# Decoder layer with a 4-bit feed-forward on one core: code tiles loaded before the rows of y, and the last batch's normalized rows made one at a time

## The reference

```python
x = x + self_attention(layernorm(x))      # 32 query heads, 16 key heads, head dim 32, causal
x = x + cross_attention(layernorm(x))     # keys and values: ctx, 4 x 64 tokens x 256, 8 kv heads, mask
x = x + down(silu(gate(n)) * up(n))       # n = layernorm(x), 1024 -> 3584 -> 1024
# gate, up, down: NF4[code] * absmax, one code per int32, one absmax per 64 codes
```

## Time and profile before

| | |
|---|---|
| median of 3 runs | 2753.37 us (2748.1 to 2753.88) |
| profiled execution | 2752.58 us, of which the span is 2750.8 us |
| busy over the span | PE 94%, DVE 75%, ACT 56%, POOL 45% |
| attention part, to the first feed-forward product | 993.7 us |
| feed-forward | 1757 us, 14 groups |
| mean granted TensorE clock | 0.971 of 2.4 GHz |

### The profile page before, as it was taken

One profiled execution on the slowest core, in us unless ns is written; L12 is line 12 of the kernel. 1 busy time (PEld: TensorE's weight loads), 2 busy tenths in 40 slices (PEclk: granted clock), 3 DMA queues, 4 the chain that ended last, 5 costly groups with the idle time before them and its releaser, 6 DMA issues.

```text
span 2750.8 us, 52702 instructions
## 1 busy us (share of the span) xinstructions
PE 2580.6 (94%) x18536; PEld 1402.1 (51%) x18536; DVE 2068.4 (75%) x2860; ACT 1548.4 (56%) x2762; POOL 1235.4 (45%) x1032
## 2 busy tenths in 40 slices
PE   5899999999975479999999999999999999999999
PEld 3567677776754444444444444444444444444444
DVE  5656777778778768878787878878787878778773
ACT  3566666666665347556464746556464746455550
POOL 2356667777765334343342424343342424243340
PEclk9999999999986689999999999999999999999999
DMA  5242443343343032111121112111111112111113
GB/s 195 93 147 93 119 131 120 98 148 107 107 154 97 28 115 69 39 58 50 45 61 38 61 46 61 38 53 53 46 59 40 61 40 66 38 53 53 46 35 122
DMA packets 155421, 212.23 MB, mean 77 GB/s; under 512 B 34576, under 2 KB 86288, under 8 KB 155280
## 3 DMA queue, kind: packets, MB, share of 16 engines
q1 hardware_dynamic: 155280, 210.31, 24.4%
HBM read 163.98 MB, written 44.56 MB: 76 GB/s over the span
## 4 chain that ended last, share of the span: by engine, by line
PE 83%; DVE 5%; DMA 3%; issue 3%; POOL 2%; ACT 2%; SPq 1%; ACTq 0%; DVEq 0%; POOLq 0%
PE bank L1728 42%; PE pair L1747 21%; PE bank L969 6%; PE bank L975 2%; PE pair L1026 2%; PE bank L997 2%; PE bank L929 1%; PE bank L1064 1%; DMA nat_parts<-nat 1%; PE pair L1049 1%; PE pair L1053 1%; PE pair L1051 1%; POOL arena L812 1%; PE bank L999 1%; PE pair L1028 1%
## 5 line engine op out<-in xcount | busy, mean ns | idle before, releaser
L277 DVE TENSOR_TENSOR w_l<-w_l 128x512 f32<-128x512 f32 x1008 | 918.9, 961 | 17.3 <-ACT w_l L260 17.2
L260 ACT ACTIVATE w_l<-proj 128x512 f32<-128x512 int32 x1008 | 592.3, 620 | 413.3 <-DVE w_l L277 299.2
L1728 PE MATMUL bank<-w_h,q_rows 128*128 128x512 f16 x2688 | 584.9, 379 | 1.2 <-issue 1.2
L1747 PE MATMUL pair<-k_rows,arena 128*128 128x512 f16 x2688 | 582.4, 379 | 0.0
L812 POOL TENSOR_TENSOR arena<-p,arena 128x512 f16<-128x512 f32 x320 | 371.5, 1169 | 230.6 <-ACT arena L1244 229.7
L1728 PEld LDWEIGHTS bank<-w_h,q_rows 128*128 128x128 f16 x2688 | 262.5, 98 | 318.4 <-issue 1.3
L1747 PEld LDWEIGHTS pair<-k_rows,arena 128*128 128x128 f16 x2688 | 262.6, 98 | 317.6
L299 POOL TENSOR_TENSOR q_rows<-x1T,q_rows 128x512 f16<-128x512 f32 x112 | 144.1, 1287 | 508.0 <-ACT q_rows L266 508.0
L257 ACT ACTIVATE w_l<-proj,bounds 128x512 f32<-128x512 int32 x336 | 231.9, 713 | 244.5 <-DVE w_l L277 209.8
L294 POOL TENSOR_TENSOR x1T<-x1T,nat 128x512 f32<-128x512 f32 x168 | 265.6, 1581 | 199.8 <-DVE x1T L283 199.8
L1438 DVE TENSOR_REDUCE block_max<-bank 128x4 f32<-128x512 f32 x320 | 218.9, 687 | 168.9 <-PE bank L999 165.4
(11 more groups left out here) (131 smaller groups left out, 3756.1 us busy)
## 6 DMA issues: line engine op xcount, KB each, us to landing
proj<-in_codes SPq DMA_DIRECT2D x168, 256.0 KB, 3.0
nat<-in_scales SPq DMA_DIRECT2D x336, 128.0 KB, 2.9
nat_parts<-nat SPq DMA_DIRECT2D x48, 256.0 KB, 2.1
q_rows<-nat_parts SPq DMA_DIRECT2D x96, 128.0 KB, 2.7
x_unit<-in_x SPq DMA_DIRECT2D x64, 128.0 KB, 2.7
x<-x_unit SPq DMA_DIRECT2D x64, 128.0 KB, 2.4
xn<-in_x SPq DMA_DIRECT2D x14, 512.0 KB, 4.3
x_row<-x SPq DMA_DIRECT2D x14, 512.0 KB, 4.6
```

The costliest lines, as they stand in the source:

```text
L260: op = self.nc.scalar.activation(self.t.line[:, m, :], self.t.codes[:, slot, :], ACT.Copy, scale=slope, bias=intercept)
L277: self.nc.vector.tensor_tensor(line[:, n + 2, :], line[:, n, :], line[:, n + 2, :], ALU.max)\
L1728: mm = nc.tensor.matmul(bank[(GATE, UP)[kind] + n % 2][:, :], w[:, chunk, kind, P * c:P * c + P], t.fT[nb][:, :, part, c, :], start=(m == ...
L1747: mm = nc.tensor.matmul(down_bank[r % 2][:, half, :], h[:, m // 3, rows], w[:, m // 3, cols], start=(m == 0), stop=(m == 5))
```

## The change

Four edits.

1. `load_late_rows` becomes `load_late_row(n)`: one of the five transfers at the start of each of the steps 59, 61, 63, 65, 67.
2. The twelve loads of y leave the end of `attention`. `load_y(sp, r)` keeps their waits, and `feed_forward` calls it twice behind the codes and scales of each of k = 1 to 6.
3. A table `LATE_ROWS` gives each of the nine late rows its iterations for stats, normalization and turn. ("cross", 3, 0) stays at -2; rows 1, 2, 3 go to turns at n = 2, 5, 9. The five third rows keep their iterations, except that the last of batch 2 has all three one later. The order of the nine, and the slot of `xn` of each (they alternate), follow from the table. SP's load of ("third", 2, 3) goes from n = 1 to n = 2.
4. In an iteration, PE transposes a row behind that iteration's scores, weighing and x_turn (cross rows were transposed ahead of the scores). ACT's high parts stand behind the exp. DVE does the low parts of a row, then a normalization, then stats, all behind mask, low part and division; before, the cross rows' stats, normalization and low parts stood ahead of them.

```diff
@@ tiles' steps, order and slots
+    LATE_STEPS = (59, 61, 63, 65, 67)
-    LN_ORDER += [("cross", B - 1, rt) for rt in range(QT)] + [("third", B - 2, QT - 1)]
-    LN_ORDER += [("third", B - 1, rt) for rt in range(QT)]
+    LATE_ROWS = [(("cross", B - 1, 0), (-2, -2, None)), (("cross", B - 1, 1), (0, 1, 2)),
+                 (("cross", B - 1, 2), (3, 4, 5)), (("third", B - 2, 3), (4, 5, 6)),
+                 (("third", B - 1, 0), (6, 7, 8)), (("cross", B - 1, 3), (7, 8, 9)),
+                 (("third", B - 1, 1), (10, 11, 12)), (("third", B - 1, 2), (14, 15, 16)),
+                 (("third", B - 1, 3), (18, 19, None))]
+    LN_ORDER += [at for at, turns in LATE_ROWS]
+    LATE_SLOTS = {at: n % 2 for n, (at, turns) in enumerate(LATE_ROWS)}
-    def third_rt(n):
-        for i, at in enumerate(((3, 4, 5), (6, 7, 8), (10, 11, 12), (14, 15, 16), (18, 19, 20))):
-            if n in at:
-                return at.index(n), LN_ORDER[len(LN_ORDER) - 1 - QT + i]
-        return None, None
+    def late_rows(stage, n):
+        return [at for at, turns in LATE_ROWS if turns[stage] == n]
@@ SP
-        def load_late_rows():
-            sp.wait_ge(turned_stored, 16 * len(STORED_ORDER))
-            sp.wait_ge(proj_done, NP * B)
-            for n, (what, b, i) in enumerate(LATE_ORDER):
-                sp.dma_start(t.fT[b][:, i, :, :, :].rearrange("p a c n -> p (a c n)"), dram["fT"][n, :, :])\
-                    .then_inc(rows_loaded, 16)
+        def load_late_row(n):
+            if n == 0:
+                sp.wait_ge(turned_stored, 16 * len(STORED_ORDER))
+                sp.wait_ge(proj_done, NP * B)
+            what, b, i = LATE_ORDER[n]
+            sp.dma_start(t.fT[b][:, i, :, :, :].rearrange("p a c n -> p (a c n)"), dram["fT"][n, :, :])\
+                .then_inc(rows_loaded, 16)
...
+            if s in LATE_STEPS:
+                load_late_row(LATE_STEPS.index(s))
...
-            if s == tiles.FIRST_STEP:
-                load_late_rows()
             load_tiles(tiles.in_step(tiles.CODES, s), tiles.in_step(tiles.SCALES, s))
...
         for n in range(-2, NX + 2):
             load_tiles(tiles.in_turn(tiles.CODES, n), tiles.in_turn(tiles.SCALES, n))
-            if n == 1:
+            if n == 2:
                 load_row("third", B - 2, QT - 1)
-        sp.wait_ge(x_added, NX * B)
-        for r in range(10):
-            sp.dma_start(t.y[r], x2_row(r)).then_inc(y_loaded[0], 16)
-        sp.wait_ge(ln_turned, 2 * len(LN_ORDER))
-        for r in range(10, 12):
-            sp.dma_start(t.y[r], x2_row(r)).then_inc(y_loaded[1], 16)
...
+    def load_y(sp, r):
+        if r == 0:
+            sp.wait_ge(x_added, NX * B)
+        if r == 10:
+            sp.wait_ge(ln_turned, 2 * last + 2)
+        sp.dma_start(t.y[r], dram["x2"][r // QT, P * (r % QT):P * (r % QT) + P, :]).then_inc(y_loaded[r // 10], 16)
...
-        def group(i, last, first=0):
-            for k in range(first, last_k(last)):
+        def group(i, last, first=False):
+            for k in range(1 if first else 0, last_k(last)):
                 tiles.load_codes(sp, i, k)
                 tiles.load_scales(sp, i, k)
+                if first and k <= 6:
+                    for r in range(2 * k - 2, 2 * k):
+                        rest.load_y(sp, r)
@@ POOL
-        ln_root(LN_AT["cross", B - 1, 1])
...
-            if n in (0, 1):
-                ln_root(LN_AT["cross", B - 1, n + 2])
...
-            stage, at = third_rt(n)
-            if stage == 0:
+            for at in late_rows(0, n):
                 ln_root(LN_AT[at])
@@ PE
-                if n in (0, 1, 2):
-                    turn(n + 1, 0)
-                    turn(n + 1, 1)
...
-                stage, at = third_rt(n)
-                if stage == 2:
-                    for half in range(2):
-                        turn(at[2], half, *at[:2])
+                for at in late_rows(2, n):
+                    turn(at)
@@ DVE
-            if n < 2:
-                rt = n + 2
-                at = LN_AT["cross", B - 1, rt]
-                dve.wait_ge(*last_loaded(rt))
-                ln_stats(at, last_row[rt])
-                if n == -2:
-                    x_low_part(LATE_X - 1, T_BANK + XT_OF, px_h, px_l)
-                ln_normal(at, last_row[rt])
-                if n == -2:
-                    x_out(LATE_X - 1, XO_BANK)
-            if 0 <= n < 4:
+            if n == -2:
+                at = ("cross", B - 1, 0)
+                turn_stats(at)
+                x_low_part(LATE_X - 1, T_BANK + XT_OF, px_h, px_l)
+                ln_normal(LN_AT[at], turn_row(at))
+                x_out(LATE_X - 1, XO_BANK)
+            if n == 0:
                 for half in range(2):
-                    ln_low_part(LN_AT["cross", B - 1, n], half, PROJ_BANK + half, xT[:, n, :, :, :])
+                    ln_low_part(LN_AT["cross", B - 1, 0], half, PROJ_BANK + half, xT[:, 0, :, :, :])
...
-            stage, at = third_rt(n)
-            if stage == 0:
-                turn_stats(at)
-            if stage == 1:
-                ln_normal(LN_AT[at], turn_row(at))
-            if stage == 2:
+            for at in late_rows(2, n):
                 for half in range(2):
                     ln_low_part(LN_AT[at], half, PROJ_BANK + half, t.fT[at[1]][:, at[2], :, :, :])
+            if n >= 0:
+                for at in late_rows(1, n):
+                    ln_normal(LN_AT[at], turn_row(at))
+                for at in late_rows(0, n):
+                    turn_stats(at)
             tiles.look_up(dve, 0, look_up_in(tiles.in_turn(tiles.OPS, n)))
```

More of the change, by code:

```diff
@@ L1123, in last_cross, with turn @@
         def last_cross():
[L1124 to L1125 removed]
+            def turn(at):
+                for half in range(2):
+                    ln_turn(LN_AT[at], half, PROJ_BANK + half)
             pe.wait_ge(x_low, LATE_X - 1)
             x_turn(LATE_X - 1, T_BANK + XT_OF, s32[:, (LATE_X - 1) % 2, :])
[L1129 to L1130 removed]
+            turn(("cross", B - 1, 0))
             pe.wait_ge(x_read, LATE_X - 1)
@@ L1396, in turn_row @@
             what, b, i = at
-            if what == "cross":
-                return x_row[:, x1_slot(i), :]
-            return last_row[i] if b == B - 1 and what == "third" else xn[:, xn_slot(*at), :]
+            if at in LATE_SLOTS and b == B - 1:
+                return last_row[i]
+            return x_row[:, x1_slot(i), :] if what == "cross" else xn[:, xn_slot(*at), :]
         def turn_stats(at):
```

34 lines of the change are left out of this document (14 added, 20 removed).

## The result

The changed kernel takes 2725.76 us (median of 4 runs, 2723.5 to 2727.71). The kernel before took 2753.01 us beside it (2748.1 to 2753.88). The ratio is 0.9904, with a 95% interval of 0.9887 to 0.9922. The profiled execution took 2724.36 us with a span of 2722.6 us, 28.2 us less than before. One more execution of the kernel before, among those that ran beside the experiments, took 3906.76 us at a mean granted clock of 0.646 and is left out of every comparison. The page of the kernel after has this for the earlier trace rows: the work is the same, and PE has less time in which to wait.

The account below looks back on a forecast made before the run. PE, busy 94% of the span, was taken as the bound, so only its idle stretches could give time. Gains of 5 + 12 + 11 = 28 us gave 2725 us; range 2718 to 2733, chance 0.64.

Parts of the forecast that it names:

- The wait and its cause: Step 60: PE idle 6.49 us for row maxima, whose transfer queued behind five stored rows; 5 us to gain.
- Up to unit 4's mask: First part of the attention's tail: 48.0 us shrinks to 26.6, so unit 4's mask starts 21.4 us earlier.
- 9.0 us were to come back: Later tail iterations: moved row work, 7.3 us, and new waits, 2.3, less 0.6, lengthen them by 9.0 us.
- The allowance of 1 us for look-ups beside GpSimd: Tail: one or two VectorE look-ups stretched by 0.54 us beside GpSimd's scaling take about 1 us.
- the rule of the Trainium skill: Tail: GpSimd contends with two-input VectorE instructions; eight look-ups stretched by 0.54 us would leave 8 us gain, not 12.
- in hand at the silu: Attention to feed-forward: first silu ready at about 1007.5, wanted by PE at 1015.5; 8 us to spare.
- the seam's lower bound: Passage from attention to feed-forward: gain of only 3 us if the first silu came 8 us later than followed.
- rival (3): Feed-forward start: lines of k = 1 wait on look-ups or scaling, 8 us later; 20 us gain, 2733; chance 0.05.
- y costs nothing: Feed-forward: ten y rows issued 56 us after PE's start, ahead of the first add_down at 86.8 us; no cost.
- (1): Tail gives little, waits at every row, and step 60's gain sinks into VectorE's load; 15 us, 2738; chance 0.16.
- (2): Tail: less idle time keeps PE at 2.4 GHz, scores and turns shrink; 37 us gain, 2716; chance 0.12.
- (4): Feed-forward: y rows land late and add_down waits; slower, 2764 us at 70 us of delay; chance 0.03.

Follow-up runs that it names:

- low parts last: Changed kernel with VectorE's low parts of late rows moved behind the iteration's normalization, statistics and look-up; 2720.48 us, tail 93.28 us.
- turns before scores: Changed kernel with PE again transposing a late row ahead of the unit's score, VectorE's new order kept; 2743.68 us, tail 113.76 us.
- second profile: The changed kernel measured again with no edit; 2724.43 us, 97.71 us from VectorE's look-ups to PE's first feed-forward product.
- the rows ahead of the masks: Changed kernel with VectorE's normalization and statistics of late rows moved ahead of the unit's mask, PE's new order kept; 2730.9 us, tail 108.05 us.

## Why the prediction was right, point by point

- **Edit 1: 5 us forecast, 5.9 measured.** The wait and its cause were as read. I had held back 1 us because VectorE might fill the place; it did not, since it had stood idle behind that wait too: its busy time between the marks is 73.30 us before and 73.44 after. The maxima had landed at 794.04 at the latest, when PE started on them, 2.3 us after SP issued them.
- **Edits 3 and 4: 12 us forecast, 12.1 measured.** (The terms gave 12.4 less 1; 12 was taken.) Up to unit 4's mask 21.4 less 1 was forecast and 20.15 came; 9.0 us were to come back and 8.0 did. That VectorE's work would stay and only its idle time go is borne out to 0.4 us. The allowance of 1 us for look-ups beside GpSimd was right as a difference, 0.8 us, but for a reason that I had not given. In the new run of look-ups the stretching is large: at the pitch of 0.60 us at which undisturbed ones follow each other six take 3.7 us and four 2.5, and they took 5.29 and 4.73, which is 3.8 us. The kernel before had nearly as much of it, in other places (its 24 look-ups took 19.8 us, the changed kernel's 20.5). But the tail did not give the 8 us that the prediction works out by the rule of the Trainium skill (GPSIMD Engine Reference, Specifications): the 4.3 us of stretching counted there for the new order are near the 3.8 measured, and the count left out that the old order paid as well.
- **Edit 2: 11 us forecast, 9.5 in that profile, 11.2 where the first 24 products were at full rate.** The step holds, with 9.0 us in hand at the silu where 8 were forecast, and the slow products behind the stall go with it: in the kernel before the granted clock was 0.50 from 1019.5 to 1028 us and 1.00 from 1030. What I left out is that the clock at the first products varies between executions: the 24 took 5.34 us in ten of the 13 profiles and 7.13, 7.22 and 7.62 in the changed kernel's first, "low parts last" and "turns before scores", which do not differ from the others there.
- **A bound that was worked out wrong.** The prediction takes 3 us as the seam's lower bound "if the silu came 8 us later than I follow it", and rival (3) uses it. With 8 us in hand that delay costs nothing; the silu would have to be some 16 us late for the gain to shrink to 3. So rival (3)'s 2733 belongs to a delay twice as long as the one it names.
- **y costs nothing:** so it was. The last of the ten rows went out 42 us after PE's start and the last pair 46 us after it, where the prediction had 56 for the ten; even all twelve in one piece cost nothing, as long as the codes of k = 1 are ahead.
- **The rivals.** (1) fell because six turns did not wait 2.8 us each; "turns before scores" shows what it would have been. (2) fell with its mechanism: the clock did not stay up (0.61 and 0.73 in the two parts, 0.57 and 0.72 before), and the tail's length did not follow it: in the changed kernel's two profiles the mean granted clock of the whole tail was 0.69 and 0.62 and the tail took 97.63 and 97.71 us. What a tail wholly at 2.4 GHz would take, no run shows. That "low parts last" reached 93 us and 2720 in total comes from a further edit and is no support for it. (3) and (4) did not happen. That the sum was met to 1 us has some luck in it: the terms were off by +0.9, +0.1 and -1.5 us, and another 0.7 us came from ahead of step 60. In the second profile the terms were 5.7, 12.1 and 11.2 us, 29.0 together, the part ahead of step 60 took 0.8 us longer than before, and the span came out the same.

Left open: why the granted clock is at its lower level at the first products in some executions and at its upper in others, with the same idle time ahead. It is not the kernel and not the length of the tail, since both levels came in the changed kernel, at 97.6 and 97.7 us.

## What to carry to other kernels

Where a chain goes round several engines, put work that is only wanted later at the end of each engine's turn, on every engine where it stands ahead of the chain: moved on PE or on VectorE alone, it left this kernel's tail 10 or 16 us longer than moved on both. Sum an engine's busy time between two marks in both kernels: if it is the same, only its waits can be the gain, and the waits that are left are the list of what to try next (here 4.4 us more). A small transfer that someone waits for belongs ahead of large ones in its queue; once it is there, it mattered neither here nor at the seam how the large ones were spread.

## What the hardware showed that I had not expected

- Both sides pay when a VectorE look-up (128x512, two SBUF inputs) runs beside a GpSimd product of that size: the look-up took up to 1.75 us in place of 0.68, the product 1.71 us in place of 1.26 (at 903.50 in the kernel before, where VectorE stood idle), and removing one such product (1.71 or 1.56 us) gave 1.07 us back.
- A normalization has one large input and pays too: it took 1.74 us at 889.24 in the kernel before and 1.75 at 908.81 with the rows ahead of the masks, each with a GpSimd scaling begun 0.07 us ahead of it, against 0.80 us for six of the seven in the changed kernel's tail (the seventh, beside the shift of L822, took 1.16).
- The first 24 products of 512 columns behind the tail took 5.34 us where the granted clock was 1.00 in their first 2 us, and 7.13 to 7.62 where it was 0.50; the 72 behind them took 15.70 us in every profile. Two executions of one kernel differed in this.
- A 4 KB transfer issued behind some 4 MB landed after 6.1 us, and after 1.7 us in the median. In the changed kernel the slowest of the 32 still took 5.2 us, at a step that I did not follow.
